# A graph and attention layer: pointwise steps and sums over K in 32x32 pieces of the array

## The reference

```python
h = batchnorm(w_qkv . xn)            # 768 channels, in 8 groups of q, k, v of 32 channels each
t = relu(h)
s = w_pw . (w_dw * t)                # per group of 32 channels: a 32x32 matrix
q, k, v = split(concat(t, s))        # 16 groups of 32 channels
out = (v k^T) q / (sum(v) + 1e-15)   # per node: v * sum(k) * q, as the sequence has one place
fx = w_res . out + b_res
x = x + graph + proj(expmap0(fx))
```

## Time and profile before

| | |
|---|---|
| median of 3 runs | 804.6 us (804.39 to 806.46) |
| the profiled execution | 804.91 us, its span 803.0 us |
| PE busy | 761.0 us (95%) |
| DVE, ACT, POOL busy | 567.7, 479.4, 414.3 us |
| mean granted clock of TensorE | 0.981 of full |

### The profile page before, as it was taken

The page is one execution under the profiler, slowest core; times in us unless marked ns, Lnnn a source line. Parts: engine busy times, 40 slices in busy tenths (PEclk is TensorE's granted clock), DMA queues, the critical chain, the costliest instruction groups (busy, mean ns, idle before and its releaser), DMA issues. The chain is left out here.

```text
span 803.0 us, 15427 instructions
## 1 busy us (share of the span) xinstructions
PE 761.0 (95%) x4960; PEld 622.9 (78%) x4960; DVE 567.7 (71%) x1623; ACT 479.4 (60%) x1113; POOL 414.3 (52%) x649
## 2 busy tenths in 40 slices
PE   6899999999899999999849999999999999999996
PEld 5678888888566666676526788888888888888885
DVE  6863488788678888888888755655666666566656
ACT  2467345989899988888728425444444444444440
POOL 3430778778458888888717712333333333333323
PEclk9999999999999999999959989999999999999999
DMA  8855122222112211212101040000000000000001
GB/s 217 208 158 161 39 58 51 59 52 53 26 32 63 59 51 35 62 25 65 42 22 38 20 130 3 27 13 26 14 27 16 24 25 16 26 14 26 16 25 38
DMA packets 35423, 41.33 MB, mean 51 GB/s; under 512 B 11520, under 2 KB 20696, under 8 KB 35339
## 3 DMA queue, kind: packets, MB, share of 16 engines
q1 hardware_dynamic: 22355, 30.71, 13.3%
q0 software_dynamic: 8000, 6.82, 3.9%
q10 hardware_dynamic: 4984, 2.79, 1.5%
HBM read 25.59 MB, written 14.60 MB: 50 GB/s over the span
## 5 line engine op out<-in xcount | busy, mean ns | idle before, releaser
L1379 PE MATMUL ps<-Z 128*125 128x256 f32 x800 | 195.5, 379 | 0.7 <-DVE L L1987 0.7
L1379 PEld LDWEIGHTS ps<-Z 128*125 128x125 f32 x800 | 149.6, 187 | 22.2 <-DVE L L1987 1.1
L1116 PE MATMUL ps<-Z,L 128*128 128x250 f32 x600 | 126.9, 373 | 0.0
L1116 PEld LDWEIGHTS ps<-Z,L 128*128 128x128 f32 x600 | 113.6, 189 | 13.2
L1007 ACT ACTIVATE Z<-Z,b1s 128x250 f32<-128x250 f32 x144 | 68.4, 503 | 78.6 <-DVE Z L1980 78.5
L1980 DVE TENSOR_TENSOR Z<-ps,L 128x250 f32<-128x250 f32 x144 | 60.1, 419 | 76.8 <-PE ps L1362 76.6
L700 POOL TENSOR_SCALAR zr<-zmv 125x1 f32<-125x1 f32 x50 | 11.5, 230 | 199.3 <-issue 189.4
L1014 ACT ACTIVATE L<-ps 128x250 f32<-128x250 f32 x144 | 54.4, 380 | 65.5 <-PE ps L1362 63.6
L1236 PE MATMUL ps<-wr,Z 128*125 128x256 f32 x400 | 92.7, 384 | 0.0
L1362 PE MATMUL ps<-L 128*128 128x250 f32 x288 | 84.0, 374 | 0.0
L852 ACT ACTIVATE Z<-Z,bn_o,bn_s 128x250 f32<-128x250 f32 x150 | 81.2, 599 | 1.0 <-DVE bn_o L1690 1.0
(11 more groups left out here) (240 smaller groups left out, 1562.7 us busy)
## 6 DMA issues: line engine op xcount, KB each, us to landing
Z<-in_x SPq DMA_DIRECT2D x25, 250.0 KB
out<-L SPq DMA_DIRECT2D x24, 250.0 KB
xt_table<-L SPq DMA_DIRECT2D x25, 231.0 KB
Z<-in_x SPq DMA_DIRECT2D x1, 2016.0 KB
g_table<-gt SPq DMA_DIRECT2D x25, 62.5 KB
gr<-g_table SPq DMA_DIRECT2D x25, 62.5 KB
Z<-in_x SPq DMA_DIRECT2D x1, 1344.0 KB
Z<-in_w SPq DMA_DIRECT2D x2, 512.0 KB, 3.3
```

The source lines that it names most:

```text
L1116: last = mm(ps[:, group_bank(n), h * BT:(h + 1) * BT], wq[:, k, c * 128:(c + 1) * 128], h_raw(b, k), start=(k == 0), stop=(k == KD - 1))
L1379: last = mm(ps[0:TP, R_BANK + t, 0:D], ge_of(b, f)[:, t * TP:(t + 1) * TP], w2s[:, f // NF, f % NF, :], start=(k == 0), stop=(k == TOP_K * ...
```

## The change

- `quarter` becomes `group`: a product on a 32x32 piece. `pointwise_kq` and `pointwise_v` have 16 products each instead of 8, `k_sums_s` 8 instead of 4. Each tile h of Q, K and V is sent from row piece i to column piece i ^ step, with steps so chosen that all sixteen pieces are used once.
- K's groups are stored in another order: tile h holds group q at place q ^ `K_TURN[h]` (1 and 3) instead of q ^ 2 in tile 0 alone. So ACT rearranges K's weights in 6 copies per half of the input channels, not 4, and the last tile of `w_res` is loaded in two halves that are swapped (3 transfers instead of 1).
- PSUM is dealt anew: each tile of s has a bank of its own (Q 0 and 1, K 2 and 3, V 5 and 6, second halves), K's sums of t are in the second halves of 0 and 1, K's sums of s in 3 and 4 from word 260, the norms in the first half of bank 4, `res` in 7, xn turned in 2.
- The waits follow: `norms(b)` waits for `attend_s(b)`; `pointwise_v(b)` for ACT's squares and copies of Q and K of b; `pointwise_kq(b)` for `attend_t(b-1)`'s first operation and `keep_xn(b-5)`; `k_sums_s(b)` for `nrm_kept(b-1)`.
- `keep_q(0)` runs ahead of the square of V's s, without its wait for the graph branch (its buffer has moved); in the branch, two half copies go and two of the last products become one.
- Behind the loop only bank numbers change, and the third pair of products of the second slot waits for a copy of the weights (`w_dve`).

The core of the diff; hunks with nothing but bank numbers are left out:

```diff
@@ -390,7 +390,7 @@
-        WQ_IN, BN_IN, PW_IN, LATE = 16 * KD, 16 * 3, 16 * 16, 16 * 3
+        WQ_IN, BN_IN, PW_IN, LATE = 16 * KD, 16 * 3, 16 * 16, 16 * 5
@@ -410,6 +410,15 @@
+        K_TURN = (1, 3)
+        Q_STEP, K_STEP, V_STEP, KST_STEP, KSS_STEP = (0, 2), (1, 3), (0, 2), (1, 3), (0, 2)
+        Q_BANK, K_BANK, SUM_BANK, NORM_BANK, V_BANK, RES_BANK = 0, 2, 3, 4, 5, 7
+        XN_BANK = K_BANK
+        KSS_AT = 260
+        assert all(KST_STEP[h] == K_TURN[h] and KSS_STEP[h] == K_TURN[h] ^ K_STEP[h] ^ Q_STEP[h] for h in range(NH))
@@ -418,7 +427,11 @@
-        HALF = 64
+        def s_of(r):
+            first = {R_Q: Q_BANK, R_K: K_BANK, R_V: V_BANK}[r]
+            return ps[:, first:first + NH, BT:2 * BT] if r == R_V else ps[:, first:first + NH, 0:BT]
@@ -434,8 +447,8 @@
-                return ps[0:TP, 6, t * D:(t + 1) * D]
-            return ps[0:TP, (R_K, R_Q)[t], 0:D]
+                return ps[0:TP, RES_BANK, t * D:(t + 1) * D]
+            return ps[0:TP, (1, 0)[t], 0:D]
@@ -783,7 +796,7 @@
-                    p = q ^ 2 if h == 0 else q
+                    p = q ^ K_TURN[h]
@@ -792,7 +805,10 @@
-                    act.dma_start(wr[:, :, :], w_res.rearrange("(k p) d -> p k d", p=128)).then_inc(late_in, 16)
+                    wr_v = w_res.rearrange("(k p) d -> p k d", p=128)
+                    act.dma_start(wr[:, 0:NO - 1, :], wr_v[:, 0:NO - 1]).then_inc(late_in, 16)
+                    for e in range(2):
+                        act.dma_start(wr[64 * e:64 * e + 64, NO - 1, :], wr_v[64 - 64 * e:128 - 64 * e, NO - 1]).then_inc(late_in, 16)
@@ -829,12 +845,13 @@
-                        for h in range(NH):
-                            for e in range(2):
-                                a_.activation(
-                                    wq[:, k, 256 * r:256 * r + 256].rearrange("p (h e q i) -> p h e q i", h=NH, e=2, i=GROUP)[:, h, e ^ 1 if h == 0 else e],
-                                    wq_raw(k).rearrange("p (h e q r i) -> p r h e q i", h=NH, e=2, r=3, i=GROUP)[:, r, h, e],
-                                    ACT.Copy).then_inc(wq_made, 1)
+                        to = wq[:, k, 256 * r:256 * r + 256].rearrange("p (h e q i) -> p h e q i", h=NH, e=2, i=GROUP)
+                        of = wq_raw(k).rearrange("p (h e q r i) -> p r h e q i", h=NH, e=2, r=3, i=GROUP)[:, r]
+                        for q in range(2):
+                            a_.activation(to[:, 0, :, q ^ 1], of[:, 0, :, q], ACT.Copy).then_inc(wq_made, 1)
+                        for q in range(4):
+                            p = q ^ K_TURN[1]
+                            a_.activation(to[:, 1, p // 2, p % 2], of[:, 1, q // 2, q % 2], ACT.Copy).then_inc(wq_made, 1)
@@ -877,22 +894,18 @@
-                    a_.activation(pair(sqs[:, r]), ps[:, 3:5, BT:2 * BT], ACT.Square).then_inc(s_sq.sem, 1)
-                else:
-                    a_.activation(sqs[:, r], ps[:, r, 0:2 * BT], ACT.Square).then_inc(s_sq.sem, 1)
+                a_.activation(pair(sqs[:, r]), s_of(r), ACT.Square).then_inc(s_sq.sem, 1)
...
-                else:
-                    act.wait_ge(edge.sem, edge.count(EARLY // 2 - 1))
-                a_.activation(sqr, ps[:, R_Q, 0:2 * BT], ACT.Relu).then_inc(q_kept.sem, 1)
+                a_.activation(pair(sqr), s_of(R_Q), ACT.Relu).then_inc(q_kept.sem, 1)
...
-                a_.activation(skr, ps[:, R_K, 0:2 * BT], ACT.Relu).then_inc(k_kept.sem, 1)
+                a_.activation(pair(skr), s_of(R_K), ACT.Relu).then_inc(k_kept.sem, 1)
@@ -945,12 +958,12 @@
-                a_.activation(nsb[qs, :], ps[qs, 5, 0:BT], ACT.Copy).then_inc(norm_kept.sem, 1)
+                a_.activation(nsb[qs, :], ps[qs, NORM_BANK, 0:BT], ACT.Copy).then_inc(norm_kept.sem, 1)
...
-                    a_.activation(h_of(b, k), ps[:, 7, k * BT:(k + 1) * BT], ACT.Copy,
+                    a_.activation(h_of(b, k), ps[:, XN_BANK, k * BT:(k + 1) * BT], ACT.Copy,
@@ -962,6 +975,7 @@
+            keep_q(0)
@@ -970,7 +984,7 @@
-                (0, keep_q),
+                (0, later(keep_q)),
@@ -1098,7 +1112,7 @@
-            pe.wait_ge(wq_made, 6 * KD)
+            pe.wait_ge(wq_made, 8 * KD)
@@ -1120,10 +1134,10 @@
-            def quarter(to, lhsT, rhs, a, e):
-                rows_, cols_ = slice(HALF * a, HALF * a + HALF), slice(HALF * e, HALF * e + HALF)
-                return mm(to[cols_], lhsT[rows_, HALF * a:HALF * a + HALF], rhs[rows_], start=True, stop=True)
+            def group(to, lhsT, rhs, i, step):
+                rows_, cols_ = slice(GROUP * i, GROUP * i + GROUP), slice(GROUP * (i ^ step), GROUP * (i ^ step) + GROUP)
+                return mm(to[cols_], lhsT[rows_, GROUP * i:GROUP * i + GROUP], rhs[rows_], start=True, stop=True)
@@ -1135,16 +1149,18 @@
-                    pe.wait_ge(att.sem, att.count(b - 1, 1))
+                    pe.wait_ge(att.sem, att.count(b - 1, 2))
+                    if b >= 5:
+                        pe.wait_ge(xn_kept.sem, xn_kept.count(b - 5))
...
-                    pe.wait_ge(z_kept.sem, 3 * NB - 7 + R_K)
+                    pe.wait_ge(z_kept.sem, 3 * NB - 4)
...
-                for h in range(NH):
-                    cq, ck = 2 * R_Q + h, 2 * R_K + h
-                    for a in range(2):
-                        quarter(bank_half(R_Q, h), pw[:, cq, :], zc(b, cq), a, a)
-                        last = quarter(bank_half(R_K, h), pw[:, ck, :], zc(b, ck), a, 1 - a)
+                for i in range(4):
+                    for h in range(NH):
+                        cq, ck = 2 * R_Q + h, 2 * R_K + h
+                        group(bank_half(Q_BANK + h, 0), pw[:, cq, :], zc(b, cq), i, Q_STEP[h])
+                        last = group(bank_half(K_BANK + h, 0), pw[:, ck, :], zc(b, ck), i, K_STEP[h])
@@ -1161,14 +1177,16 @@
-                    pe.wait_ge(att.sem, att.count(b - 1, 2))
...
-                    pe.wait_ge(z_kept.sem, 3 * NB - 3)
-                for h in range(NH):
-                    cv, ck = 2 * R_V + h, 2 * R_K + h
-                    for a in range(2):
-                        last_v = quarter(bank_half(4 - h, 1), pw[:, cv, :], zc(b, cv), a, a ^ h)
-                        last_k = quarter(bank_half(3 + h, 0), bo, zc(b, ck), a, 1 - (a ^ h))
+                    pe.wait_ge(z_kept.sem, 3 * NB - 1)
+                pe.wait_ge(s_sq.sem, s_sq.count(b, 2))
+                pe.wait_ge(k_kept.sem, k_kept.count(b))
+                pe.wait_ge(q_kept.sem, q_kept.count(b))
+                for i in range(4):
+                    for h in range(NH):
+                        cv, ck = 2 * R_V + h, 2 * R_K + h
+                        last_v = group(bank_half(V_BANK + h, 1), pw[:, cv, :], zc(b, cv), i, V_STEP[h])
+                        last_k = group(bank_half(Q_BANK + h, 1), bo, zc(b, ck), i, KST_STEP[h])
@@ -1180,12 +1198,13 @@
-                    pe.wait_ge(att.sem, att.count(b - 1))
+                    pe.wait_ge(att.sem, att.count(b - 1, 1))
+                    pe.wait_ge(nrm_kept.sem, nrm_kept.count(b - 1))
...
-                for a in range(2):
-                    last_0 = quarter(bank_half(1, 0), bo, skr[:, 0:BT], a, a)
-                    last_1 = quarter(bank_half(2, 0), bo, skr[:, BT:2 * BT], a, 1 - a)
+                for i in range(4):
+                    last_0 = group(ps[:, SUM_BANK, KSS_AT:KSS_AT + BT], bo, skr[:, 0:BT], i, KSS_STEP[0])
+                    last_1 = group(ps[:, NORM_BANK, KSS_AT:KSS_AT + BT], bo, skr[:, BT:2 * BT], i, KSS_STEP[1])
@@ -1199,29 +1218,30 @@
+                    pe.wait_ge(att.sem, att.count(b, 1))
...
-                        last = mm(ps[32 * i:32 * i + 32, 5, 0:BT], ones[:, 0:32], sqo[:, i * BT:(i + 1) * BT], start=True,
+                        last = mm(ps[32 * i:32 * i + 32, NORM_BANK, 0:BT], ones[:, 0:32], sqo[:, i * BT:(i + 1) * BT], start=True,
...
-                            last = mm(ps[32 * q:32 * q + 32, 5, 0:BT], ones[:, 0:32], of, start=(i == 0), stop=(i == 3),
+                            last = mm(ps[32 * q:32 * q + 32, NORM_BANK, 0:BT], ones[:, 0:32], of, start=(i == 0), stop=(i == 3),
...
-                        last = mm(ps[96:128, 5, 0:BT], ones[:, 0:32], sqo[:, i * BT:(i + 1) * BT], start=(i == 0),
+                        last = mm(ps[96:128, NORM_BANK, 0:BT], ones[:, 0:32], sqo[:, i * BT:(i + 1) * BT], start=(i == 0),
...
-                    last = mm(ps[0:TP, 5, 256 + 2 * t:258 + 2 * t], nsb[:, t * TP:(t + 1) * TP], (sel if b < NB else sel_o)[:], start=True,
+                    last = mm(ps[0:TP, NORM_BANK, 256 + 2 * t:258 + 2 * t], nsb[:, t * TP:(t + 1) * TP], (sel if b < NB else sel_o)[:], start=True,
@@ -1247,7 +1267,7 @@
-                        last = nc.tensor.transpose(ps[:, 7, k * BT + t * TP:k * BT + (t + 1) * TP],
+                        last = nc.tensor.transpose(ps[:, XN_BANK, k * BT + t * TP:k * BT + (t + 1) * TP],
@@ -1349,6 +1369,8 @@
+                if n == P2 and g == 1:
+                    pe.wait_ge(w_dve, 1)
@@ -1725,15 +1747,16 @@
```

(40 more changed lines are left out.)

12 lines of the change are left out of this document (6 added, 6 removed).

## The result

| | before | after |
|---|---|---|
| median | 805.3 us (804.39 to 806.46, 4 runs) | 819.6 us (818.74 to 819.71, 3 of 4 runs) |
| ratio | | 1.0173, 95% interval 1.0152 to 1.0194 |
| the profiled execution, its span | 804.91, 803.0 us | 818.74, 816.9 us |
| PE, DVE, ACT, POOL busy | 761.0, 567.7, 479.4, 414.3 us | 750.3, 568.5, 477.7, 415.7 us |

One of the four runs of after took 1567.35 us and is in neither the range nor the ratio.

The account below looks back on a forecast made before the run. It took TensorE's own work to set the loop's pace, with every engine nearly full. Regular blocks +8.0, block 0 +2.1, the dividing branch -0.6 and the front +0.2 gave +9.7 us: 814.3 us for the median, range 806.5 to 823.0.

Parts of the forecast that it names:

- a loop of 9.39 us: Attention loop: `norms` waiting for `attend_s` makes each regular block 9.39 us instead of 8.92; +8.0 us over 21 blocks.
- The late blocks don't stay late: Blocks 1 to 12: the gather moves 1.2 us ahead, so `make_u` ends 6.76 behind `norms`, not 7.43.
- D: Rival, regular blocks: late blocks stay late, +16.0 instead of +8.0, 822.3 us; chance within the 0.78 of the `attend_s` loop.
- Block 0: Loop's first block: `norms(0)` 2.4 us later, through `keep_q(0)` and the wait for `attend_s(0)`; +2.1 us (1.5 to 2.6).
- The front: Before the loop: 12 weight copies instead of 8 and three `w_res` transfers instead of one; +0.2 us (0 to 1.4).
- The block that divides: Block 20's branch, with block 21: two half copies go, three last products become two; -0.6 us (-1.3 to 0).
- TensorE's own saving, 0.64 a block: Attention loop: 0.32 us saved in each of `pointwise_kq` and `pointwise_v`, nothing in `k_sums_s`; TensorE's work falls to 8.28.
- The bad end: Small pieces on TensorE: at 23 ns per instruction, 64 would take 1.5 us instead of 0.85.
- Rival A: Attention loop: the wait is hidden and the pieces pay, period 8.28, 15.4 us go, 790.9 us; chance 0.10.
- B: Rival: the loop is as short as in block 17 everywhere, edges kind; +1.9 us, 806.5 us; chance 0.05.
- C: Rival, attention loop: small pieces issue slowly, period 11.3, 855 us, or 880 if row pieces run singly; chance 0.07.
- Four row pieces on one bank: TensorE's products: by the skill's rule they would run one after another; the trace disagreed for two, undecided for four.

Follow-up runs that it names:

- the gather's place: GpSimd's gather put ahead of `scale_of_u`, against the changed kernel with the norms in bank 5: 803.4 us, ratio 0.998 to before.
- `check_s` in the middle: `check_s` put between the two operations of `attend_t`, against the changed kernel with the norms in bank 5: 802.1 us, ratio 0.9956 to before.

## Why the prediction was right, and where it was off

- **The wait in `norms` closes a loop of 9.39 us.** Right, and shown both ways: taken out of the change, 16.4 us go; put into the kernel before, 16 come. The order of the waits was right, and the size came close: `make_u` ends 5.74 to 7.67 behind `norms`, 6.76 in the mean of the 21 regular blocks, the number taken from blocks 13 to 19 of the earlier trace rows. That the mean agrees to the hundredth is luck: nine of these blocks stand at about 6.4, less than any of the rows that gave 6.76, and ten at 6.8 to 7.7. The period came out as 9.48. What was under-sized is the way from VectorE to TensorE: 0.21 us in most blocks and up to 0.37, where the earlier trace rows gave 0.15 (+1.5 over 21 blocks), and block 1, where `attend_s` waits for K's sums (+0.5).
- **The late blocks don't stay late.** Right: the last scale comes 2.6 behind `norms` in ten of the blocks 2 to 19 and 3.2 at the latest; D is out. The `make_u` that are late now, 7.1 to 7.7 behind in blocks 13, 15, 17 and 19, have another cause, a part of which is below: a small operation ahead of them (L1831) takes 0.65 to 0.72 us there.
- **Block 0.** `norms(0)` started 2.2 us later counted from the 768-channel product, forecast 2.4. The step that failed is that a moved start was the only cost: the wait for `keep_q(0)` leaves TensorE idle, and the granted clock fell to 0.50, +1.7 us. The forecast priced the wait and not what the engine does right behind it.
- **The front**: forecast 0.2, and by experiment 0 within 1.8 us. By that the +1.9 of the traces is not of the change.
- **The block that divides**: -2.0 instead of -0.6. The two copies are 0.64 of it, as forecast. Beside them `make_x1` ahead of the division starts 0.6 earlier (2.62 against 3.25 behind `norms`), `attend_s` waits 0.10 for K's sums instead of 0.68, and `norms(21)` took 1.89 where it took 2.67 at a falling clock. The shorter wait is of the small pieces: it is 0.11 at most in every kernel that has them and 0.68 in every one that doesn't. The earlier `make_x1` goes with the new wait (2.6 to 2.8 in the four kernels with it, 3.05 to 4.1 in the others). In other kernels `norms(21)` took between 1.89 and 3.56, so the clock's part is not of the change.
- **TensorE's own saving, 0.64 a block.** The step for `pointwise_kq` was right: 32 instructions in two rounds, 0.71 us instead of 1.08. `pointwise_v` too: K's sums start 0.44 behind it instead of 0.89. Wrong was "nothing" for `k_sums_s`: 0.90 instead of 0.60 us. The quick blocks of the kernel without the wait take 8.41 to 8.52, not 8.28. The bad end that I had from the rows, 23 ns for each instruction with the weight loads counted, was the right kind of cost in the wrong place: it isn't the first 32 products' instructions that go slowly but those behind them.
- **Rival A** would have been wrong even without the wait. 790.9 counted the whole 0.64 in all 24 blocks. 803.2 was measured: 0.2 a block. A part of the rest is lost to `k_sums_s` (0.3 a block). What keeps the mean at 8.81, 0.3 to 0.4 over the quick blocks, is in the main VectorE's late `make_u` and `attend_t`, and through GpSimd the scales that they wait for; this is read from the rows and not isolated by a run, and the one edit aimed at it (the gather's place) gained nothing. With `check_s` in the middle the mean is 8.67. B, C and D fall with their numbers.
- **Four row pieces on one bank.** In `pointwise_kq` sixteen instructions, four on each of four banks and each of these four from another row piece, start within 0.11 us. The Trainium skill, "TensorEngine Tiling (Array Packing)", section "Restrictions and Gotchas", says that different row tiles cannot access the same PSUM bank simultaneously; the trace disagrees for four as it did for two. Each of the four writes another 32 partitions here; that row pieces may share both bank and partitions, no run tries.

The sum was 4.1 us under the profiled execution: 1.7 of it the front, 1.8 block 0, 2.0 the regular blocks and the step to block 1, less 1.4 in the block that divides. By the medians, 814.3 and 819.6, it was 5.3 under.

## What to carry to other kernels

When engines' shares of busy time are close, ask of an added wait which loop it closes and add up that loop; the faster engine's savings then only turn into its waiting time. Before two tiles share a bank, ask what order their readers and writers get tied into: here the same pieces win, if by 0.2% only, with the norms one bank further on. And of a wait on TensorE count, beside its length, what may run behind it at the lower clock.
